# Local attention in a decoder layer: half of the transposed keys copied out of PSUM by ScalarE, and loops placed and shortened

## The reference

```python
h = shift_token(x)                       # half of the channels moved on by one position
q, k, v = split(h @ wqkv)                # 8 heads of 64
q = l2norm(q) * qs;  k = l2norm(k) * ksc
q, k = rotary_xpos(q, k)
o = local_attention(q, k, v)             # window 64: each block of 64 sees itself and the block before, softmax
x = x + o @ wo
h = layernorm(shift_token(x)) * lg + lb
a, g = split(h @ w1 + b1)
x = x + (a * gelu(g)) @ w2 + b2
```

## Time and profile before

| | us |
|---|---|
| median of 3 runs | 1828.15 (1822.93 to 1831.68) |
| the profiled execution | 1827.18 |
| its span, first to last instruction | 1825.1 |
| TensorE busy | 1705.1 (93%) |
| ScalarE busy | 1415.4 (78%) |
| VectorE busy | 1012.2 (55%) |
| GpSimd busy | 453.6 (25%) |

### The profile page before, as it was taken

The page is one execution under the profiler, slowest core; times in us unless marked ns, Lnnn a source line. Parts: engine busy times, 40 slices in busy tenths (PEclk is TensorE's granted clock), DMA queues, the critical chain, the costliest instruction groups (busy, mean ns, idle before and its releaser), DMA issues. The chain is left out here.

```text
span 1825.1 us, 67884 instructions
## 1 busy us (share of the span) xinstructions
PE 1705.1 (93%) x27988; PEld 1021.4 (56%) x27988; DVE 1012.2 (55%) x3114; ACT 1415.4 (78%) x2635; POOL 453.6 (25%) x385
## 2 busy tenths in 40 slices
PE   7898899999998999999999978999989879999888
PEld 4674455555554555555555435666663346666633
DVE  5455533334342334333333058999975489999854
ACT  4343599999998999999999956888873369889842
POOL 1114000000000000000000027777830077877400
PEclk9898899999999999999999999999999989999999
DMA  2000311111111111111101030111110001111100
GB/s 60 3 1 26 107 49 51 62 44 63 63 49 45 55 44 63 63 56 57 49 31 44 3 110 18 33 36 32 23 36 11 0 18 32 25 34 32 33 15 35
DMA packets 47439, 73.56 MB, mean 40 GB/s; under 512 B 8401, under 2 KB 38225, under 8 KB 47185
## 3 DMA queue, kind: packets, MB, share of 16 engines
q1 hardware_dynamic: 47184, 69.85, 12.4%
HBM read 21.08 MB, written 2.10 MB: 13 GB/s over the span
## 5 line engine op out<-in xcount | busy, mean ns | idle before, releaser
L689 ACT ACTIVATE x_probs<-x_pss 128x1024 f32<-128x1024 f32 x832 | 806.3, 1021 | 54.8 <-PE x_pss L610 39.8
L624 PE MATMUL x_acc<-x_probs,x_v 128*32 128x256 f32 x6656 | 438.5, 381 | 0.0
L610 PE MATMUL x_pss<-x_qx,x_kx 32*128 32x256 bf16 x9984 | 350.8, 271 | 12.8 <-issue 5.7
L610 PEld LDWEIGHTS x_pss<-x_qx,x_kx 32*128 32x128 bf16 x9984 | 222.6, 93 | 200.0 <-ACT x_probs L689 180.5
L624 PEld LDWEIGHTS x_acc<-x_probs,x_v 128*32 128x32 f32 x6656 | 206.9, 110 | 93.4 <-issue 9.3
L736 DVE COPY x_vnext<-x_psp 128x128 f32<-128x128 f32 (+1 forms) x199 | 59.2, 297 | 316.5 <-PE x_psp L588 312.3
L1289 ACT ACTIVATE l_prob<-l_neg_sim,l_neg_top 128x128 f32<-128x128 f32 x512 | 198.2, 395 | 6.0 <-DVE l_neg_top L1180 6.0
L917 POOL TENSOR_TENSOR l_turned_half<-l_raw,l_tabB 128x512 f32<-128x512 f32 x128 | 185.8, 1473 | 50.4 <-ACT l_raw L1248 50.0
L665 POOL COPY x_zq<-zT 128x256 f32 (+1 forms) x15 | 6.0, 400 | 763.8 <-PE x_psp L595 693.6
L1180 DVE CUSTOM_DVE_ANT_0 l_neg_sim<-l_pss,w_window,l_inv_norm 128x128 f32<-128x128 f32 x512 | 148.8, 347 | 6.2 <-issue 5.5
L927 POOL TENSOR_TENSOR l_direct<-l_direct,l_turned_half 128x1024 f32<-128x1024 f32 x64 | 151.9, 2374 | 0.0
(11 more groups left out here) (184 smaller groups left out, 2593.6 us busy)
## 6 DMA issues: line engine op xcount, KB each, us to landing
x_kx<-x_kp SPq DMA_DIRECT2D x96, 208.0 KB, 2.3
x_cT<-in_context SPq DMA_DIRECT2D x16, 832.0 KB, 4.6
x_qx<-x_qp SPq DMA_DIRECT2D x48, 192.0 KB, 3.0
l_vmid<-l_vt SPq DMA_DIRECT2D x64, 128.0 KB, 2.3
xT<-in_x SPq DMA_DIRECT2D x8, 256.0 KB, 4.6
shifted<-zT SPq DMA_DIRECT2D x32, 64.0 KB, 2.0
hs<-zT SPq DMA_DIRECT2D x32, 64.0 KB, 2.0
out_x<-xT SPq DMA_DIRECT2D x8, 256.0 KB, 2.0
```

Of the source, the lines that this page charges most:

```text
L610: ins = pe.matmul(pss[bank(k, 2 * p + r // 2)][:, r % 2, e, :], kx[par][rows, g, j * P:(j + 1) * P], qx[par][rows, g, a * S:(a + 1) * S], ...
L624: ins = pe.matmul(acc[32 * r:32 * r + 32, 0:S], v[:, j, g, r, :], probs[SLOT[p]][r // 2][:, r % 2, e, :], start=(u == 0), stop=(u == UNITS ...
L689: act.activation(probs[SLOT[p]][y][:, :, :, :], pss[bank(k, 2 * p + y)][:, :, :, :], ACT.Sigmoid, scale=HD ** -0.5).then_inc(weighed, 1)
```

## The change

VectorE's turn loses `place_keys(later(x, 1), 0)`; ScalarE gets a `place_keys` of its own and calls it with t = 0 between `copy(x, 0, 0)` and `place_queries(later(x, 1), 1)`. VectorE's `place_keys` (t = 1 from the turns) gets one more wait, on `placed_k`. The loops of `turns` hold two turns on GpSimd, VectorE and ScalarE (6 passes) and four on TensorE (3 passes, as now). The loops of `turns`, of `chunks` and of the gelu on ScalarE are made with `aligned_loop`, which places the first instruction of the loop at slot 0 of a block of code.

```diff
--- before.py
+++ after.py
@@ -34,6 +34,11 @@
 HID = 341
 HC = (HID + P - 1) // P
 FAR = 3.0e38
+
+
+def aligned_loop(nc, eng, times):
+
+    return nc.Fori(0, times, engines=bass.OrderedEngineSet([eng.engine]), head_slot={eng.engine: 0})
 
 
 def shift_in(sp, shifted, zT, landed, n):
@@ -857,13 +862,13 @@
             n, r, q = x
             return n + by, (r + by) % 4, q + (r + by) // 4
 
-        def turns(eng, body):
+        def turns(eng, body, per):
 
             for n in range(-2, 2):
                 body((n, n % 4, n // 4))
-            with eng.Fori(0, 3) as i:
-                for k in range(2, 6):
-                    body((4 * i + k, k % 4, i + k // 4))
+            with aligned_loop(nc, eng, (B - 4) // per) as i:
+                for k in range(2, 2 + per):
+                    body((per * i + k, k % 4, i + k // 4))
             for n in range(B - 2, B + 1):
                 body((n, n % 4, n // 4))
 
@@ -948,7 +953,7 @@
             pool.memset(moved_to[64:P, :].rearrange("p (b s) -> p b s", s=S)[:, :, 0:1], 0.0).then_inc(first_cleared, 1)
             pool.wait_ge(first_cleared, 1)
             pool.wait_ge(ready, 2)
-            turns(pool, turn)
+            turns(pool, turn, 2)
 
         @block.tensor
         def _(pe):
@@ -1101,7 +1106,7 @@
                 flip_k(later(x, 1), 1)
                 project_v(later(x, 1), 0)
 
-            turns(pe, turn)
+            turns(pe, turn, 4)
 
         @block.vector
         def _(dve):
@@ -1110,6 +1115,7 @@
                 if exists(x):
                     n, r, _ = x
                     dve.wait_ge(flipped_k, 2 * n + t + 1)
+                    dve.wait_ge(placed_k, 2 * n + t)
                     dve.tensor_copy(kT[r % 2][:, :, t * P:(t + 1) * P],
                                     psk[:, :, :].rearrange("p (h e) d -> p h (e d)", e=2)).then_inc(placed_k, 1)
 
@@ -1215,7 +1221,6 @@
                 mask(x, 1, 1)
                 multiply_k(later(x, 2), 1)
                 norm(x, 0, 1)
-                place_keys(later(x, 1), 0)
                 add(later(x, -1))
                 norm(x, 1, 0)
                 place_keys(later(x, 1), 1)
@@ -1229,7 +1234,7 @@
                                   w[scales][:, :, :].rearrange("p m d -> p (m d)").unsqueeze(1).broadcast_to([P, 2, 2 * FD]),
                                   ALU.mult).then_inc(ready, 1)
             dve.wait_ge(ready, 2)
-            turns(dve, turn)
+            turns(dve, turn, 2)
 
         @block.scalar
         def _(act):
@@ -1271,6 +1276,14 @@
                     act.wait_ge(flipped_q, 2 * n + t + 1)
                     act.activation(qT[r % 2][:, :, t * P:(t + 1) * P],
                                    psq[:, :, :].rearrange("p (h e) d -> p h (e d)", e=2), ACT.Copy).then_inc(placed_q, 1)
+
+            def place_keys(x, t):
+
+                if exists(x):
+                    n, r, _ = x
+                    act.wait_ge(flipped_k, 2 * n + t + 1)
+                    act.activation(kT[r % 2][:, :, t * P:(t + 1) * P],
+                                   psk[:, :, :].rearrange("p (h e) d -> p h (e d)", e=2), ACT.Copy).then_inc(placed_k, 1)
 
             def copy_out(x, b):
                 if exists(x):
@@ -1317,10 +1330,11 @@
                 exps(x, 1, 0)
                 squares(later(x, 2), 1)
                 copy(x, 0, 0)
+                place_keys(later(x, 1), 0)
                 place_queries(later(x, 1), 1)
 
             act.preload_act_table_set("natural_log_exp_and_others")
-            turns(act, turn)
+            turns(act, turn, 2)
 
 
 def norm_and_gate(nc, tag, norms, gates, zT, hs, w, moved, layer, xT=None, out=None, stored=None, next_shift=None):
@@ -1368,7 +1382,7 @@
         def chunks(eng, body):
 
             body(0, 0)
-            with eng.Fori(0, NCH // 2 - 1) as i:
+            with aligned_loop(nc, eng, NCH // 2 - 1) as i:
                 for u in range(2):
                     body(2 * i + 1 + u, 1 - u)
             body(NCH - 1, 1)
@@ -1524,7 +1538,7 @@
             guess(1)
             act.preload_act_table_set("gelu_and_others")
             act.wait_ge(bias_ready, layer + 1)
-            with act.Fori(0, NCH) as n:
+            with aligned_loop(nc, act, NCH) as n:
                 for c in range(HC):
                     act.wait_ge(up, passes + HC * n + c + 1)
                     act.activation(gelu[c][:, :], psg[c][:, :], ACT.Gelu,
```

## The result

| | before | changed |
|---|---|---|
| median of 4 runs, us | 1827.61 (1822.93 to 1831.68) | 1866.71 (1858.57 to 1872.08) |
| ratio, with its 95% interval | | 1.0211 (1.0166 to 1.0256) |
| the profiled execution, us | 1827.18 | 1872.08 |
| its span, us | 1825.1 | 1870.3 |

The change makes the kernel about 2% slower: 2.1%, with an interval of 1.7 to 2.6. The forecast was 1862 us, slower, in a range of 1852 to 1884. The lines of the changed kernel are shifted by 5 or more: the keys' copy is L1119 on VectorE and L1285 on ScalarE, `flip_k` L1025, `score` L1041, `turn_over` L1054, `add` L1207, `norm` L1197 and L1199, `mask` L1186.

What follows compares the result with a forecast made beforehand. VectorE, 97% busy, set the pace at 16.32 us a turn, with a dependence loop through TensorE and ScalarE near. Profiled 1827.18 plus 26 turns x 1.33 = 34.6, loops 0, gave 1861.8, predicted as 1862 us; range 1852 to 1884.

Steps and rivals of the forecast that it cites:

- The ring of dependences: Attention loop, mask through TensorE, ScalarE, flip and VectorE to the next mask: late copy grows it from 16.32 to 17.65 us.
- T0: End of `mask(x,0,1)` on VectorE, the point from which the forecast timed one turn of the attention loop.
- How many turns: Turns 1 to 13 in each of two layers pay the delay: 26 turns x 1.33 = 34.6 us.
- turn 14: Last attention turn with the moved copy; no squares and no wait in `copy_k`, so no loss was counted.
- The loops, taken as 0: Shorter, placed loops were priced at 0, as turns back in the kernel before showed no cost; range -1 to +8 us.
- the bound of 8 us: Upper limit for the loops' cost: each entry of four stages waits for one code block, 2.0 us each.
- Rival 1: VectorE's relief arrives in the attention loop: 28 turns x 0.60 = 16.8 us less, 1810 us; chance 0.07.
- the 0.60: Time in us per attention turn that VectorE is spared by giving up the first key half's copy.
- 1 us that placement could give back: Lower limit for the loops: one irregular `norm` of 1.80 us, 0.90 over usual, might be the code's doing.
- All its own work: VectorE's queue from its second key copy to the next mask takes 2.44 us, with no waiting in it.
- Rival 2: Turns back stall: five in each of two layers cost one 2.0 us fetch each, 1882 us; chance 0.08.
- Rival 4: TensorE's clock falls in the attention loop from the new stops: about 1.2 us a turn, 31 us, 1893 us; chance 0.03.

Runs made afterwards that it cites:

- the copy alone: Kernel before with only the first key half's copy moved to ScalarE as in the change, loops as before: 1861.48 us, ratio 1.0199.
- the loops alone: Kernel before with only the loops changed as in the change, both key copies staying on VectorE: 1828.18 us, ratio 1.0011.
- the kernel with the second half moved: Kernel before with the second key half's copy moved to ScalarE behind the second `place_queries`, the first staying on VectorE: 1839.83 us, ratio 1.0085.
- GpSimd cut: Kernel before without the first key half's copy on any engine, and GpSimd's products and join cut to one or two of sixteen heads: 1823.48 us.
- both copies behind the exponentials: Kernel before with ScalarE doing the first key half and second `place_queries` right behind block 1's exponentials, ahead of the squares: 1821.83 us, ratio 0.9990.

## Why the prediction was right, step by step

- **The ring of dependences** (T0, TensorE, ScalarE's copy, the second flip, VectorE's copy, the mask) held as written. From T0 to ScalarE's copy: 1179.08 - 1170.16 = 8.92 us, taken as 9.02. From the copy's end (1179.08 + 0.59 = 1179.67) to the flip at 1179.81: 0.14, the value taken between 0.05 and 0.24. From the flip to VectorE's copy 0.67, as taken. Growth of a turn: 1.33 forecast, 1.31 over nine turns (17.63 against 16.32).
- **How many turns.** 34.6 us forecast, 36.3 measured for the copy alone. That they lie so close is partly luck, since the turns themselves hold less: 32.5 us in the profile of the copy alone (above). Twelve steps a layer have the full growth or nearly (15.65 in layer 2 of the changed kernel); the thirteenth, where 1.33 was counted, grew from 13.89 to 14.75, by 0.86; and turn 14, for which the forecast took none, costs 0.70 (12.37 to 13.07). The turns ahead of the loop lose nothing in the copy alone, as forecast: 52.2 us from the first matmul of the stage to the first `add`, 52.6 before.
- **The loops, taken as 0.** In the medians about 2 us, not told from none, so the price holds; the reasoning doesn't. It read all turns of the kernel before as alike at 16.32, where one in layer 1 is 17.57, and looked for a price at the turns back. The stops lie elsewhere: 1.6 to 1.9 us on VectorE at the entry in layer 1, and in the profiled execution the clock of 0.64 behind it, which made the entry turn 21.28. Beside it the turn of 17.57 goes away. Of the span, the changed kernel's profile has 8.4 us more than that of the copy alone; 3.8 are in the loop of layer 1, 0.3 in that of layer 2, 3.3 between the layers, where executions differ by as much anyway. That this is near the bound of 8 us is luck. The mark "gated layers unchanged at 88" failed (89.3 and 91.3), but by the clock, as in the copy alone.
- **Rival 1** had the right doubt for half of the reason. The order of waits stopped it in the changed kernel; but with the order mended it still doesn't arrive, since 0.54 of the 0.60 goes into the norm. The forecast saw that this norm could be stretched, and called it hidden. In the changed kernel it is; in the kernels without the delay it is not. The bound of "1 us that placement could give back" was the same thing: the norm of 1.80 us ends 0.55 behind a GpSimd instruction. It isn't the place of its code; but in the kernels with placed loops no turn of 17.57 occurs (16.33 in the loops alone), which gives back 1.24 us beside the stop at the entry. The Trainium skill (Perfetto Trace Analysis, section Optimizing Scalar/DVE Operations) proposes the move when VectorE is saturated. At 97% busy it was, and the same move takes the time to 1.0199 or 1.0019 of before by its place in ScalarE's queue, and to 0.9990 with the queries' copy moved too.
- **"All its own work"**, the 2.44 us from VectorE's copy to the mask, had a twin: in the kernel before, `score` ended 0.32 us before the mask started (1203.48 + 1.16 = 1204.64, against the mask's memset at 1204.96, below), and 0.32 is also the distance where the mask did wait for it, in the kernel with the second half moved (1216.51 to 1216.83). So both paths were full, and with VectorE's own shortened (GpSimd cut) the mask did wait, 0.17. The row of the kernel before:

```profile
1204.96 0.06 DVE L1178 MEMSET l_beat<- 128x1 f32 x1
```

- **Rival 2** was wrong in the changed kernel (its turns back cost nothing). Stops at turns back of the size that it named did show elsewhere, in an unplaced loop with one call moved: 2.25 us on VectorE, and a turn of 21 us. **Rival 4** didn't come in the changed kernel's regular turns; with the copy 0.48 us later it did, in every second turn.
- Of the marks named beforehand: `add` every 17.5 to 17.8, yes (17.55 to 17.72); 40 us before the flip, yes; VectorE idle over 1 us, yes (1.22); VectorE near 87%, no, 90%, because its norms got longer: 867 ns in the mean on the page's group, 760 before.

Nothing here beats the kernel before by a margin that can be told; the best, both copies behind the exponentials, is 0.9990 (0.9966 to 1.0014).

## What to carry to other kernels

Before moving work to an engine with slack, ask at what time in its queue that engine comes to it and who waits for the result; the same copy cost 36 us or some 3 by two places in the order. A full engine that is relieved gains only up to the next limit, and here there were two close by, a GpSimd instruction that holds up the next operation and the wait of the mask for its score; leaving the work out altogether is the quick way to see what a move could bring at best. When loops are changed, read the first turn in the loop and the turns back one by one, and judge the loop by medians, since one profiled execution overstated it. And before a longer stretch is put down to an edit, look at its granted clock and at the same stretch in kernels without the edit.

## What the runs showed of the hardware

- VectorE's norm, which has two SBUF inputs, ends 0.55 us behind the end of the GpSimd instruction that runs when it starts: 0.92, 1.23 or 1.80 us in place of 0.69, by how much was left of it, and 0.69 where some 0.1 was left. With GpSimd's instructions cut short it was 0.69 to 0.72 throughout.
- TensorE's granted clock stayed at 1.00 with a stop of 1.52 us in every turn of 17.6, and fell (0.91 over the turn) in every second turn with stops of 2.00 in turns of 18.0 to 19.4. A single stop of 2.03 us was followed by 0.64 over 4 us. The same gated layer took 88.4 us at a mean clock of 0.99 and 91.8 at 0.96, in kernels with either kind of loop.
- Loops whose heads are placed went with a stop at the entry in layer 1, of VectorE (1.6 to 1.9 us) in four kernels and of ScalarE (2.3) in the fifth, and of GpSimd (2.7 to 2.8) in all five; in layer 2 VectorE had none that long. A stop of VectorE of 2.2 to 2.4 in the gated layers went with placed loops of two turns alone, and cost no time that can be seen (88.44 us with it, 88.41 without). A loop that isn't placed cost nothing at its turns back in the kernel before, and 2.25 us on VectorE, then 3.5 on TensorE, at both of those of layer 2 in one that differs by a single call.
